# A decoder layer on one core: who clears the later stacks, second gate banks, warm-up matmuls, and new orders

## What is computed

```python
x = x + linear_attention(layernorm(x))      # 16 heads of 8, phi = elu + 1, projection with bias
x = x + cross_attention(layernorm(x), ctx)  # causal softmax, 16 heads of 8, 256 x 256 scores
x = x + ffn(layernorm(x))                   # below

scores = sigmoid(h @ Wr)                          # 8 experts, the best 2, weights normalised
routed = sum(cw[e] * ((silu(h @ Wg[e]) * (h @ Wu[e])) @ Wd[e]) for e in range(4))
routed += (cw[4] + cw[6]) * h + cw[7] * relu(h)   # expert 5 gives nothing
ffn = routed + causal_conv4(h)
```

## Time and profile before

| | us |
|---|---|
| median of 3 runs | 180.59 (180.39 to 182.45) |
| the profiled execution | 180.98 |
| its span, first to last instruction | 179.1 |
| busy in the span: PE, DVE, ACT, POOL | 159.0, 141.6, 126.9, 87.9 |

### The profile page before, as it was taken

One profiled execution on the slowest core, in us unless ns is written; L12 is line 12 of the kernel. 1 busy time (PEld: TensorE's weight loads), 2 busy tenths in 40 slices (PEclk: granted clock), 3 DMA queues, 4 the chain that ended last, 5 costly groups with the idle time before them and its releaser, 6 DMA issues.

```text
span 179.1 us, 7215 instructions
## 1 busy us (share of the span) xinstructions
PE 159.0 (89%) x2682; PEld 117.8 (66%) x2682; DVE 141.6 (79%) x464; ACT 126.9 (71%) x283; POOL 87.9 (49%) x171
## 2 busy tenths in 40 slices
PE   6999497887888989999999999999799999998663
PEld 6978365564566766776788667877377668675343
DVE  2335979999976999999899899889878765868831
ACT  7266379673974768977866888847947879974670
POOL 4534667325103411356364275142744475698893
PEclk9999879999999999999999999999999999999999
DMA  5557113220332321320330133122310001010102
GB/s 133 175 207 224 40 48 96 73 60 18 93 76 49 80 66 37 91 63 9 81 91 18 38 76 78 35 62 51 77 37 29 7 6 31 2 33 0 33 0 59
DMA packets 19594, 11.11 MB, mean 62 GB/s; under 512 B 3188, under 2 KB 19188, under 8 KB 19560
## 3 DMA queue, kind: packets, MB, share of 16 engines
q1 hardware_dynamic: 19368, 10.26, 21.7%
q0 software_dynamic: 192, 0.39, 0.8%
HBM read 3.10 MB, written 1.05 MB: 23 GB/s over the span
## 4 chain that ended last, share of the span: by engine, by line
PE 62%; ACT 10%; issue 9%; DMA 6%; POOL 4%; DVE 4%; SPq 3%; ACTq 0%; POOLq 0%; DVEq 0%
PE self_bank L939 13%; PE pv_bank L939 12%; PE max_pair L939 8%; PE cross_bank L939 7%; PE soft_pair L939 7%; PE ffn_bank L939 7%; DMA bproj_all<-bproj_dram 4%; ACT probs L641 3%; PE self_bank L943 2%; SPq L363 2%; PE pv_bank L1115 2%; DMA qs<-qparts 1%; ACT hidT L711 1%; ACT vs L634 1%; DVE negmax L832 1%
## 5 line engine op out<-in xcount | busy, mean ns | idle before, releaser
L832 DVE TENSOR_REDUCE negmax<-max_pair 128x4 f32<-128x1024 f32 (+3 forms) x56 | 49.9, 915 | 6.8 <-PE max_pair L939 6.7
L641 ACT ACTIVATE probs<-soft_pair 128x1024 f32<-128x1024 f32 x40 | 41.1, 1027 | 9.8 <-PE soft_pair L939 9.3
L475 POOL TENSOR_TENSOR rstd<-vareps,exponent 128x2 f32<-128x2 f32 x24 | 17.2, 719 | 29.0 <-DVE vareps L747 28.7
L939 PE MATMUL pv_bank<-probs,vs 128*32 128x128 f32 (+3 forms) x512 | 19.0, 301 | 0.2 <-DVE x L864 0.2
L516 POOL TENSOR_TENSOR shared<-shared,tapped 128x256 f32<-128x256 f32 x24 | 17.6, 733 | 2.2 <-ACT tapped L675 1.5
L939 PEld LDWEIGHTS pv_bank<-probs,vs 128*32 128x32 f32 x512 | 13.4, 110 | 5.7 <-issue 1.8
L939 PE MATMUL max_pair<-ks,qs 64*64 64x128 bf16 (+3 forms) x512 | 15.9, 230 | 0.0
L939 PE MATMUL soft_pair<-qs,ks 64*64 64x128 bf16 (+3 forms) x512 | 15.8, 230 | 0.0
L939 PE MATMUL max_pair<-later_key,eye 64*64 64x128 bf16 (+1 forms) x224 | 11.2, 237 | 4.6 <-DMA qs<-qparts 1.4
L939 PEld LDWEIGHTS max_pair<-later_key,eye 64*64 64x64 bf16 x224 | 5.3, 105 | 11.4 <-issue 5.0
L524 POOL TENSOR_TENSOR hid<-hraw,cw 128x256 f32<-128x256 f32 x16 | 9.8, 613 | 5.4 <-DVE hraw L917 4.0
(11 more groups left out here) (182 smaller groups left out, 409.8 us busy)
## 6 DMA issues: line engine op xcount, KB each, us to landing
ks<-kparts SPq DMA_DIRECT2D x45, 64.0 KB, 2.0
qs<-qparts SPq DMA_DIRECT2D x45, 64.0 KB, 2.1
out_dram<-result SPq DMA_DIRECT2D x8, 128.0 KB, 1.9
ctxin<-ctxT_dram SPq DMA_DIRECT2D x1, 896.0 KB, 10.8
xin<-x_dram SPq DMA_DIRECT2D x1, 768.0 KB, 12.8
W<-weights_dram SPq DMA_DIRECT2D x1, 710.5 KB, 6.0
qs<-maxparts SPq DMA_DIRECT2D x32, 4.0 KB
xin<-x_dram SPq DMA_DIRECT2D x2, 128.0 KB, 2.5
```

What stands on the lines that cost most here:

```text
L475: nc.gpsimd.tensor_tensor(t["rstd"][b.par][:, :], t["vareps"][:, :], exponent[:, :], ALU.pow).then_inc(rstd_done[n], 1)
L641: nc.scalar.activation(probs[b.par][u][:, :, :], soft_pair[:, :].rearrange("p (r x) -> p r x", r=2), ACT.Exp).then_inc(exp_done, 1)
L832: nc.vector.tensor_reduce(negmax[:, :, first:first + n, t], of_unit(max_pair, 64 * t + 64, n, at), AX.X, ALU.max, negate=True).then_inc(ma ...
L939: return nc.tensor.matmul(out, lhsT, rhs, start=start, stop=stop, skip_group_check=True)
```

## The change

Four parts.

1. The clears of stacks 1 and 2 (`clear.0.1`, `.2`, `.4`, `.5`) leave ACT and become GpSimd memsets, which count a semaphore of their own; stack 0 stays with ACT. Writers of later stacks wait for that one.
2. For batches 5, 6 and 7 the second half of `ffn_gate_up` goes to a bank of `max_pair` or `soft_pair`, whose last use is over, and waits for that instead of `times_up`.
3. The last weighing (`hid.7.1`) moves from POOL to DVE.
4. Ten warm-up matmuls are added: five behind `cross_v.0`, one behind `self_sum.1`, two each behind `cross_norm_t.0` and `self_x_t.2`.

All five orders are written anew; steps move by some places nearly everywhere, but each list keeps its steps apart from the above.

```diff
 "sp":
-        mid_q.0.0 hi_k.1.0 hi_q.1.0 mid_q.1.0 mid_k.1.0 send_max.0.0 mid_q.2.0 hi_k.2.0 mid_k.2.0 hi_q.2.0 send_max.1.0
+        mid_q.0.0 mid_k.1.0 hi_k.1.0 hi_q.1.0 mid_q.1.0 hi_k.2.0 send_max.0.0 hi_q.2.0 mid_q.2.0 mid_k.2.0 send_max.1.0
...
 "pool":
-        eye.0.0 pattern.0.0 ones.0.0 ones.0.1 rstd1.0.0 rstd1.1.0 heads.0.0 bias.0.0 bias.1.0 lo_k.0.0 causal.0.0
-        rstd2.0.0 rstd1.2.0 rstd1.3.0 rbias.0.0 bias.2.0 lo_q.0.0 rstd2.1.0 bias.3.0 lo_k.1.0 lo_q.1.0 rstd2.2.0
+        heads.0.0 pattern.0.0 ones.0.0 rstd1.0.0 rstd1.1.0 ones.0.1 eye.0.0 clear.0.1 causal.0.0 clear.0.4 bias.0.0
+        clear.0.2 bias.1.0 clear.0.5 rstd2.0.0 rstd1.2.0 rstd1.3.0 lo_q.0.0 lo_k.0.0 rstd2.1.0 lo_k.1.0 rstd1.4.0
...
 "act":
-        clear.0.0 clear_v.0.0 xnT.0.0 act_q.0.0 clear.0.3 xnT.1.0 act_kv.0.0 act_q.1.0 hi_k.0.0 act_kv.1.0 mid_k.0.0
+        clear_v.0.0 xnT.0.0 act_q.0.0 clear_v.0.1 xnT.1.0 act_kv.0.0 hi_k.0.0 act_q.1.0 clear.0.0 clear.0.3 mid_k.0.0
...
 "dve":
-        reduce.1.1 stats2.3.0 var2.3.0 reduce.1.2 norm2.3.0 reduce.1.3 phi_k.4.0 reduce.1.4 phi_q.4.0 kvsum.4.0
-        max_mid.1.0 div1.4.0 var1.5.0 stats1.6.0 reduce.2.0 div1.4.1 norm1.5.0 div1.4.2 rest_q.3.0 reduce.2.1 div2.0.0
+        reduce.1.1 stats2.3.0 var2.3.0 reduce.1.2 rest_k.3.0 phi_q.4.0 reduce.1.3 phi_k.4.0 reduce.1.4 kvsum.4.0
+        norm2.3.0 var1.5.0 div1.4.0 max_mid.1.0 stats1.6.0 div1.4.1 reduce.2.0 div1.4.2 norm1.5.0 var1.6.0 reduce.2.1
...
-        gate.6.1 route.7.0 route.7.1 times_up.6.1 route.7.2 route.7.3 gate.7.0 times_up.7.0 route.7.4 route.7.5
-        route.7.6 route.7.7 gate.7.1 times_up.7.1 finish.6.0 finish.7.0
+        route.6.7 gate.6.1 route.7.0 route.7.1 route.7.2 times_up.6.1 route.7.3 gate.7.0 times_up.7.0 route.7.4
+        route.7.5 route.7.6 route.7.7 gate.7.1 times_up.7.1 hid.7.1 finish.6.0 finish.7.0
 "pe":
-        self_x_t.0.0 self_q1.0.0 self_x_t.1.0 self_kv.0.0 self_q1.1.0 cross_k.0.0 self_sum.0.0 self_kv.1.0 self_out.0.0
-        cross_v.0.0 self_o_t.0.0 self_sum.1.0 self_proj.0.0 self_out.1.0 cross_norm_t.0.0 self_x_t.2.0 cross_q2.0.0
+        self_x_t.0.0 self_q1.0.0 self_x_t.1.0 self_kv.0.0 cross_k.0.0 self_q1.1.0 self_sum.0.0 self_out.0.0 self_kv.1.0
+        self_o_t.0.0 self_proj.0.0 cross_v.0.0 self_sum.1.0 cross_norm_t.0.0 cross_q2.0.0 self_out.1.0 self_x_t.2.0
...
-        ffn_hid_t.5.0 ffn_down.5.0 ffn_gate_up.6.1 ffn_x_t.7.0 ffn_router.7.0 ffn_gate_up.7.0 ffn_hid_t.6.0
-        ffn_gate_up.7.1 ffn_down.6.0 ffn_hid_t.7.0 ffn_down.7.0
+        ffn_gate_up.6.0 ffn_gate_up.6.1 ffn_down.5.0 ffn_x_t.7.0 ffn_router.7.0 ffn_gate_up.7.0 ffn_gate_up.7.1
+        ffn_hid_t.6.0 ffn_down.6.0 ffn_hid_t.7.0 ffn_down.7.0
...
+        WARM_AFTER = {("cross_v", 0): 5, ("self_sum", 1): 1, ("cross_norm_t", 0): 2, ("self_x_t", 2): 2}
...
+        def cleared_for(b):
+            return (cleared, 2) if b.c == 0 else (later_cleared, min(2 * b.c, 4))
+        def gate_bank(b, t):
+            if t == 0 or b.c < B - 3:
+                return bank_of("ffn", b)[:, :]
+            return (max_pair[:, 0:512], max_pair[:, 512:1024], soft_pair[:, 0:512])[b.c - (B - 3)]
...
-                    sp.wait_ge(cleared, min(2 * b.c + 2, 6))
+                    sp.wait_ge(*cleared_for(b))
...
+            def clear(_, what):
+                tile, value = (ks[what], BF16_ONES) if what < 3 else (qs[what - 3], 0.0)
+                nc.gpsimd.memset(tile[:, :, :].rearrange("r h s -> r (h s)").bitcast(f32), value).then_inc(later_cleared, 1)
...
+            def weigh_last(b, t):
+                dve.wait_ge(hid0_done, b.count(2, t + 1))
+                dve.wait_ge(route, b.count(ROUTE, ROUTE))
+                dve.wait_ge(pe_hid_t, b.count(1, -1))
+                nc.vector.tensor_tensor(hid[b.par][:, t, :].rearrange("p (e i) -> p e i", e=EM),
...
+                    warm(WARM_AFTER.get((step.__name__, b.c), 0))
...
             def ffn_gate_up(b, t):
                 if t == 0:
                     pe.wait_ge(tanr_done, b.count(1, 1))
+                elif b.c < B - 3:
+                    pe.wait_ge(hid0_done, b.count(2, 1))
+                elif b.c < B - 1:
+                    pe.wait_ge(max_read, PER_BATCH * B)
                 else:
-                    pe.wait_ge(hid0_done, b.count(2, 1))
-                mm(bank_of("ffn", b)[:, :], x3T[b.par][:, KC - 1 + t * P:KC - 1 + (t + 1) * P], w_gate_up).then_inc(pe_gate_up, 1)
+                    pe.wait_ge(exp_done, SOFT_N * B)
+                mm(gate_bank(b, t), x3T[b.par][:, KC - 1 + t * P:KC - 1 + (t + 1) * P], w_gate_up).then_inc(pe_gate_up, 1)
```

More of the change, by code:

```diff
@@ L63 @@
[L63 to L66, removed]
-        exp.0.4 hi_q.3.0 outT.0.0 exp.1.0 mid_q.3.0 hi_k.4.0 o2T.0.0 exp.1.1 o1T.4.0 exp.1.2 exp.1.3 xnT.5.0 max_hi.2.0
@@ L96 @@
-        route.0.2 reduce.3.4 gate.0.0 x2.1.0 times_up.0.0 route.0.3 max_mid.3.0 x1.5.0 route.0.4 var1.7.0 route.0.5
-        route.0.6 stats2.5.0 rest_k.5.0 route.0.7 stats3.1.0 var2.5.0 gate.0.1 reduce.4.0 times_up.0.1 norm2.5.0
-        reduce.4.1 var3.1.0 phi_q.6.0 reduce.4.2 div2.2.0 rest_q.5.0 norm3.1.0 div2.2.1 phi_k.6.0 reduce.4.3 finish.0.0
-        norm1.7.0 kvsum.6.0 reduce.4.4 div1.6.0 div1.6.1 div1.6.2 max_mid.4.0 rest_k.6.0 x2.2.0 reduce.5.0 route.1.0
-        x1.6.0 stats2.6.0 route.1.1 reduce.5.1 var2.6.0 route.1.2 stats3.2.0 route.1.3 norm2.6.0 var3.2.0 gate.1.0
@@ new lines @@
+        rest_k.5.0 gate.0.0 route.0.2 reduce.3.4 x2.1.0 route.0.3 x1.5.0 route.0.4 max_mid.3.0 stats2.5.0 var2.5.0
+        var1.7.0 route.0.5 times_up.0.0 norm2.5.0 route.0.6 stats3.1.0 reduce.4.0 route.0.7 var3.1.0 reduce.4.1
+        rest_q.5.0 gate.0.1 times_up.0.1 phi_k.6.0 reduce.4.2 phi_q.6.0 kvsum.6.0 rest_k.6.0 reduce.4.3 div2.2.0
+        div2.2.1 div1.6.0 reduce.4.4 norm3.1.0 finish.0.0 div1.6.1 max_mid.4.0 div1.6.2 norm1.7.0 reduce.5.0 x2.2.0
+        x1.6.0 stats2.6.0 route.1.0 reduce.5.1 var2.6.0 stats3.2.0 route.1.1 var3.2.0 route.1.2 reduce.5.2 route.1.3
@@ L128 @@
-        soft.2.2 max.3.4 o_proj.1.0 cross_k.5.0 self_o_t.5.0 soft.2.3 maxrow.3.0 self_proj.5.0 ffn_gate_up.0.1
-        self_x_t.6.0 soft.2.4 max.4.0 pv.2.0 pv.2.1 cross_v.5.0 soft.3.0 max.4.1 self_q1.6.0 cross_norm_t.5.0 out_t.2.0
-        ffn_hid_t.0.0 max.4.2 soft.3.1 cross_q2.5.0 self_kv.6.0 max.4.3 soft.3.2 ffn_down.0.0 o2_t.2.0 self_sum.6.0
-        cross_k.6.0 max.4.4 soft.3.3 self_out.6.0 ffn_x_t.1.0 o_proj.2.0 maxrow.4.0 ffn_router.1.0 self_o_t.6.0 max.5.0
-        soft.3.4 self_proj.6.0 cross_v.6.0 max.5.1 pv.3.0 pv.3.1 self_x_t.7.0 ffn_gate_up.1.0 self_q1.7.0
@@ new lines @@
+        max.4.2 soft.3.0 out_t.2.0 cross_k.6.0 self_sum.6.0 ffn_hid_t.0.0 max.4.3 soft.3.1 self_out.6.0 cross_v.6.0
+        max.4.4 soft.3.2 ffn_down.0.0 maxrow.4.0 o2_t.2.0 soft.3.3 max.5.0 self_o_t.6.0 ffn_x_t.1.0 o_proj.2.0
+        self_proj.6.0 ffn_router.1.0 max.5.1 soft.3.4 pv.3.0 pv.3.1 max.5.2 soft.4.0 self_x_t.7.0 ffn_gate_up.1.0
+        self_q1.7.0 max.5.3 cross_norm_t.6.0 self_kv.7.0 cross_q2.6.0 out_t.3.0 max.5.4 soft.4.1 ffn_gate_up.1.1
+        cross_k.7.0 self_sum.7.0 o2_t.3.0 soft.4.2 maxrow.5.0 cross_v.7.0 o_proj.3.0 self_out.7.0 ffn_hid_t.1.0 soft.4.3
```

170 lines of the change are left out of this document (91 added, 79 removed).

## The result

The changed kernel takes 181.59 us in the median of 6 runs (180.58 to 183.16) against 180.49 for the kernel before: a ratio of 1.0118, 95% interval 1.007 to 1.0165. Within two per cent it is the same, but it is slower, and the forecast of 178.2 (range 175.6 to 181.2) is missed on the other side. A second set of 12 runs on another chip gave 181.73, ratio 1.0076 (1.0035 to 1.0117). The ratios leave disturbed runs out, the medians do not.

The account below looks back on a forecast made before the run. TensorE was taken to bound the kernel from 54.49 to 122.70 us, so gains had to come from outside it. Terms -0.7 - 0.8 + 0.3 - 0.3 - 0.9 = -2.4 us gave 178.2, range 175.6 to 181.2.

Parts of the forecast that it names:

- the saturated stretch: Behind `max.2.0`, where TensorE is nearly always busy: only misfits can enter, +0.3 us, between 0 and 2.2.
- the tail: Behind the last `pv`: `gate_up.7.1` in its own bank and `hid.7.1` on VectorE bring the end forward, -0.9 us.
- The clears: Four fills on GpSimd, 1.1 us each, hidden before `rstd2.0`, which then waits for VectorE alone: no cost.
- The first term: Up to `max.0.0` and the first reduction: batch 0 first brings both forward, -0.7 us.
- Up to `max.2.0`: From `max.0.0` to `max.2.0`: a stall goes through earlier stack writes and reductions shift, -0.8 us.
- The warm-ups hidden, the clock full: Early TensorE waits: nine of ten warm-ups hidden, one may delay 0.2 us; no clock slice under 9 from 18 to 27.
- "-0.3": The stall before `max.7.0`: more TensorE work behind `cross_q2.7` shortens the wait, -0.3 us, at most 1.4.
- the three gate steps: `gate_up` second halves of batches 0 to 2, waiting for `times_up`: 0.1 us left for batch 0, 0.35 for batch 2.
- what comes out of the early part is kept: Ahead of 54.49 us: time won there stays won, because the full stretch then only starts earlier.
- the base: Whole kernel: the sum starts from the profiled execution of 180.98 us, 0.4 above the median of 180.59.
- what is won early is lost on TensorE: Rival: the gate steps of batches 0 to 2 stall in full, +2.2 us, giving 180.3; chance 0.20.
- the last: Sign of being wrong: a longer stretch between `max.2.0` and the last `pv`.

Follow-up runs that it names:

- e1: The kernel before with only the ten warm-up matmuls added: 181.99 us, ratio 1.0154.
- e2: The kernel before with only the second gate banks and `hid.7.1` on VectorE, `ffn_gate_up.7.1` ahead of `ffn_hid_t.6`: 178.78 us, ratio 0.9973.
- e4: The kernel before up to `max.2.0`, then the changed kernel's orders with second gate banks and `hid.7.1` on VectorE: 183.45 us, ratio 1.0244.
- e8: e1 with the two zero writes of batch 3 moved from SyncE's queue to GpSimd's: 179.99 us, ratio 1.0006.
- e12: e8 with e2's tail (second gate banks, `hid.7.1` on VectorE): 179.66 us, ratio 0.9982.
- e9: The changed kernel once more, for a second profile: 181.73 us.
- e13: The changed kernel with the two zero writes of batch 3 moved to GpSimd's queue: 182.4 us, ratio 1.0129.
- e6: The changed kernel without the ten warm-ups: 182.28 us, interval 1.005 to 1.018.
- e11: e3 with e2's tail and the two zero writes of batch 3 in GpSimd's queue: 179.33 us, ratio 0.9978.
- e10: The changed kernel up to `max.4.0`, then the order of before, keeping its tail parts: 181.45 us, interval 1.0056 to 1.0142.
- e14: The changed kernel with late words reordered, among them `mid_k.5`, `lo_k.5`, `norm2.6`, `finish.2` and `hidT.7`: 181.07 us, ratio 1.005.
- e3: The changed kernel's clears, warm-ups and orders up to `max.2.0`, then the order of before, one gate bank, `hid.7.1` on GpSimd: 181.28 us, ratio 1.012.
- e5: e3 without the ten warm-ups: 181.97 us, interval 1.0042 to 1.0132.
- e7: e3 with e2's tail and without the ten warm-ups: 182.15 us, interval 1.006 to 1.0191.

## Why the prediction was wrong

Which term failed is seen by adding up the first profile against that of the kernel before: -1.56 to `max.0.0`, -0.80 to `max.2.0`, +0.14 to `max_mid.2`, +1.82 to the last `pv` and -0.05 to `finish.7`, -0.45 in all, where the sum had -2.4. The two terms that failed are the saturated stretch and the tail; the early part won more than was forecast, and it is in part luck.

**Right.** The clears: 0.95 us each, forecast 1.1; `rstd2.0` at 16.7, waiting for VectorE alone. No norm lay beside a clear, as forecast. The first term: -1.56 at `max.0.0`, of which 0.69 is that `self_x_t.0` started at 5.84 and not 6.53 (the first eleven warm-ups took 4.31 us and not 5.07; this start lies between 5.6 and 6.5 in the profiles of either order, so it is not the change); -0.87 remain, forecast -0.7. Up to `max.2.0`: a further -0.80, forecast -0.8, and this agreement is luck. The stall of 0.95 that the term removes was mostly one execution's: in e1, e2, e4, e8 and e12, with the list of before, this stretch takes 24.24 to 24.72, and not the 25.07 of the kernel before's profile. With the new list it takes 24.26 or 24.27 in the changed kernel, e9 and e13, so the change wins 0 to 0.5 there. The warm-ups hidden, the clock full: yes, in the profiles of this order; in the order of before five of them stood in front of `self_o_t.0`, which came 1.1 later behind `cross_v.0` (e1). One reading was loose: in the earlier trace rows TensorE is at nine tenths from slice 16 to 36, but for slice 29.

**Wrong, first: the saturated stretch, "+0.3".** Together with the "-0.3" for `max.7.0`, which lies in the same cut, the forecast for the middle stretch was 0. Measured +1.8 in the first profile, +1.1 in e9, +0.6 in e13, +0.9 in e6 and +1.3 in e4, though the stall before `max.7.0`, 1.38, came down to 0.4 or less: the term was mis-sized. I followed only the three gate steps, and none of them stalls. The recurring waits are others: `max.5.0` (0.43, 0.88, 0.87 in the changed kernel twice and in e4), `cross_norm_t.6` (0.47, 0.46) and `max.7.4` (0.54). Nearly every word of the later lists had moved, and I priced the three whose code I was reading; I also asked only what TensorE would wait for, and the chain of the changed kernel runs through VectorE. That the later order as a whole costs is shown by e13 against e11 and by e4 against e2; how the sum falls on its words is not: e10 and e14 only moved it.

**Wrong, second: the tail, "-0.9".** Measured -0.05. The part that I argued is real: with the order of before it gives 0.43 (21.40 to 21.38 against 21.83 and 21.82 in the table). The new order takes 0.37 of it back, in all five of its profiles. The sum had `base.7` on GpSimd come out level with `finish.7`; here it ends 21.69 behind the last `pv` (21.54 in the kernel before, 20.95 in e2), and `finish.7` waits for it. `hidT.7` behind `skip.7` on ScalarE is seen in the rows too; e14 put it ahead, but then `skip.7` and with it `base.7` came later still (22.29), so its price is not shown.

**Wrong, third: "what comes out of the early part is kept".** In e1, e3, e5 and e7 it was given back within one batch, at `max.3.0`. The table of stretches shows TensorE busy and so hides that SyncE's queue ran level with it: in the kernel before the fourteen writes were issued from 55.42 to 65.23, and `max.3.0` came at 66.89 with no wait. The changed kernel shows no such wait, since `pv.1` stands ahead of `max.3.0` there; it did not lose its lead by this.

**Wrong, fourth: the base.** The sum was made against one execution of 180.98 as though it were typical. It had a half clock from 21.3 to 24.7 (two of its rows are in the earlier trace rows) and two stalls that the same program halves in e2. Of 104 runs of the kernel before in these series 28 show a mean granted clock of 1.00, and their median is 178.9; 45 show 0.99, with 180.2; 31 show 0.98 or less, with 181.0. Of the 18 of the changed kernel ten show 1.00, with 181.0; eight less, with 182.8. In the kernel before a mean clock of 0.99 goes with 1.3 us more than one of 1.00. So the base of the sum carried that much which a run of it need not have, and a part of the early gain was only this. The profiles of the changed kernel, 180.58 and 180.12, lie 1.0 and 1.6 under the medians of their sets (and that of e13, 180.44, lies 2.0 under): of the 2.1 us between the runs that keep their clock, about 1.1 is the middle stretch of the profiles, and the early gain counts against it; the rest is seen in none of them, and its cause stays open.

Of the rivals, "what is won early is lost on TensorE" was the right one in kind, with 180.3; its places were wrong and its price too low. Of the signs of being wrong the last came true: from `max.2.0` to the last `pv` the first profile takes 2.0 us longer.
